# A two-way decaying scan by matrix products over channels, in place of DVE's scans, in a gated RWKV and FFN block

## The chip, the cores and the metric

One NeuronCore of one Trainium2 chip. The metric is the device time of one execution in microseconds, from which a median over several executions is taken. A profiled execution gives the rows below.

## The reference

`x` and `ctx` are 32 sequences of 128 tokens and 256 channels, float32. The attention part is a bidirectional accumulation with a decay per channel, on `k = v = ctx`, and the FFN is a gated one on fake-quantised integers.

```python
ek = exp(k); ew = exp(w)                      # w, u: one value per channel
# forward:  A_t = sum_{i<t} ew^(t-1-i) ek_i v_i ;  B_t the same without v ; backward alike
cur = exp(u + k)
wkv = (Af + Ab + cur * v) / (Bf + Bb + cur)
x = x + tanh(g_xattn) * sigmoid(layernorm(x)) * wkv
xq = fake_quant(layernorm(x))                 # one scale: the maximum over all of x
h = fake_quant(silu(xq @ wg.T) * (xq @ wu.T)) # weights fake-quantised by row; one scale for all h
x = x + tanh(g_ffn) * (h @ wd.T)
```

Two maxima over everything cut the work into three stages: attention and layernorms, then gate and up, then down.

## The kernel before

The engines' programs are written out by hand, each in its own block, and wait for each other on counting semaphores. Only the first stage and the weights' preparation are changed.

- **First stage, by groups.** A group is 4 sequences (`GS`), `GROUPS` = 8. A half (`h`) is 128 of the 256 channels, so there are 16 units of 128 partitions by 512. The loop of every engine is skewed by hand over groups (`step(g)`).
- For a unit, ACT takes `ek = exp(ctx)` (L410), POOL multiplies it by ctx (`pk`, L315), PE transposes both into PSUM so that channels are partitions and tokens lie along the free dimension (`turn_in`, L867), ACT makes `cur` (L421), and DVE runs two scans of 1024 elements, forward (L664) and backward (L666). POOL clears the borders (`zero`, L325). PE transposes cur and both scans back, accumulating the three in one bank (`turn_out`: L881, L883, L885), once for e and once for p.
- DVE makes the denominator `(1 + exp(-norm x)) * sum_e` (L677), ACT its reciprocal by Ln and Exp (L443, L446), DVE the `mixed` term (L689), POOL adds it to x (`residual`, L334).
- **Layernorms.** `stats1` and `join1` (L623, L632) on x before the residual, `rstd1` on POOL (L342 to L348), `exp_z` on ACT (L432, four instructions a group). After the residual `stats2`, `join2` (L643, L652), `rstd2` on POOL (L354 to L361), `normalise` on ACT (L457, four a group), `turn_z` on PE (L903), `keep_z` on ACT (L466), `peak_z` on DVE (L696). All of it is inside the same skewed loop, one to three groups behind.
- **Weights.** `weight_scales` (DVE L611 to L613), `quantise_weights` (L474), `cast_weights` (L482) on ACT, `turn_weights` (PE, L918), `keep_weights` (ACT L491). Gate and up are done in the first groups, down behind the gate and up stage.
- **Behind the last group** `global_peak` (DVE L751, PE L944, DVE L754 to L756) gives the scale, `quantise_x` (DVE L766) and `cast_x` (ACT L547) the integers, and L976 is the first gate matmul. L1012 is the down product, L841 its scaling, L990 the product of `ones` with a diagonal, the only float32 matmul that is no transpose.

Of the kernel before, what the change touches and what calls it, by code (L numbers as in the profile page):

```python
# [40 lines left out]

def gated_rwkv_ffn(nc, x, ctx_kv, g_xattn, g_ffn, w, u, clip_x, clip_down, w_gate, w_up, w_down, out):
# [14 lines left out]
    SCW = 2 * UNIT + 2  # L57
    assert T == P and IR == P // 2 and UNIT == 512 and CH == 2 and GROUPS >= 5

    with ExitStack() as stack:  # L60
# [5 lines left out]

# [10 lines left out]
        ones = sb("ones", [P, P])  # L77
        small = sb("small", [P, 64])
# [5 lines left out]

        hidden = sb("hidden", [P, BLOCKS * HB])
        at = [0]

        def part(cols):
            at[0] += cols
            assert at[0] <= BLOCKS * HB  # L90
            return hidden[:, at[0] - cols:at[0]]

        ctx_all = part(SEQS * C)
        ek = part(2 * UNIT).rearrange("p (s n) -> p s n", s=2)
        pk = part(2 * UNIT).rearrange("p (s n) -> p s n", s=2)
        cur = part(4 * UNIT).rearrange("p (s q n) -> p s q n", s=2, q=2)
        scans = part(2 * 2 * SCW).rearrange("p (s d n) -> p s d n", s=2, d=2)

        decay = [tile.rearrange("p (h n) -> p h n", h=CH) for tile in (
            part(CH * 2 * UNIT), xq[:, :, :, :, :].rearrange("p a b c d -> p (a b c d)").bitcast(F32))]  # L100
        ez = part(GC)

        den = part(2 * UNIT).rearrange("p (s n) -> p s n", s=2)
        lnd = part(UNIT)
        rden = part(2 * UNIT).rearrange("p (s n) -> p s n", s=2)

        late = silu_out[:, :, :].rearrange("p s n -> p (s n)")
        mixed = late[:, 0:2 * UNIT].rearrange("p (s n) -> p s n", s=2)
        z = late[:, 2 * UNIT:2 * UNIT + GC]
        x8 = sb("x8", [P, 2, CH, 512], I8)  # L110
        h8_space = sb("h8_space", [P, 2 * HB // 4])

        z_flat = z_t[:, :, :].rearrange("p h n -> p (h n)")
        WC = KA * C
        w_nat = [z_t[:, 0, TOK - WC:TOK], z_t[:, 1, TOK - WC:TOK], h8_space[:, 0:WC]]
        w_int = sb("w_int", [P, WC], I8)
        w_intb = sb("w_intb", [P, WC], BF16)
        assert TOK - WC >= 4 * UNIT

# [6 lines left out]

        ps = stack.enter_context(nc.psum_tensor("ps", [P, 8, 512], F32))
        TURN = 6, 6, 2


# [8 lines left out]

        EVEN = (KA + 1) // 2  # L140
        ODD = KA // 2

# [4 lines left out]


# [3 lines left out]
        wu_raw = small[:, 16:20]  # L152
# [17 lines left out]
        nr2 = sb("nr2", [P, GS])  # L170
        mr2 = sb("mr2", [P, GS])
        consts = sb("consts", [P, 3, GS])
        zero_tile = sb("zero_tile", [P, 2, 2 * GS + 1])
        zeros = zero_tile[:, :, :]


# [866 lines left out]
```

## Time and profile before

| | |
|---|---|
| median of 3 runs | 245.43 us (242.9 to 245.86) |
| the profiled execution | 245.59 us, its span 243.9 us |
| busy share of the span: DVE, ACT, PE, POOL | 90%, 68%, 64%, 50% |
| first stage, until the first gate matmul | 0 to 153.0 us |
| gate and up with their maximum | 153.0 to 208.6 us |
| down product and output | 208.6 to 243.9 us |

Times in rows are microseconds from the start of the span, those of one instruction in nanoseconds where the view says so. PE is the matmul engine and PEld its weight loads. The granted TensorE clock is a share of 2.4 GHz, so that 0.50 is 1.2 GHz. A window's columns are the engine's busy time with the number of instructions in it.

### The profile page before, as it was taken

What the parts mean: (1) busy time and instruction counts of PE and PEld (TensorE: products, weight loads), DVE (VectorE), ACT (ScalarE), POOL (GpSimd) and SP (SyncE); (2) the same over time, 40 slices, a digit from 0 to 9 for tenths busy, and PEclk for the clock granted to TensorE, in tenths of its full rate; (3) what the DMA queues carried; (4) which work ended last, traced back from release to release, by engine and by line L of the source; (5) the groups of instructions that cost most, each with busy time, mean ns of one, the idle gap of its engine ahead of it and who ended that gap; (6) DMA issues with size and microseconds to landing.
All of it is one profiled execution on the core that took longest, in us unless ns stands there. A gap on an engine that the chain in (4) does not pass through costs nothing.

```text
span 243.9 us, 3531 instructions
## 1 busy us (share of the span) xinstructions
PE 156.2 (64%) x1002; PEld 113.4 (47%) x1002; DVE 219.0 (90%) x307; ACT 166.8 (68%) x220; POOL 121.4 (50%) x151
## 2 busy tenths in 40 slices
PE   0609675476726596556565622999595993689970
PEld 0409565476625485545465612434232341466640
DVE  0999999999999999999999787279999799899993
ACT  5454975929959197393772759799797788689700
POOL 7431444438465384454832740057373575008992
PEclk9955979889999978999987875699998899599995
DMA  5796566610000000000000000000000000002358
GB/s 152 217 336 198 174 203 219 220 50 4 0 0 0 0 0 0 0 0 0 0 0 0 4 0 0 0 1 0 3 0 0 0 0 0 1 3 86 129 180 293
DMA packets 16107, 15.08 MB, mean 62 GB/s; under 512 B 2016, under 2 KB 15840, under 8 KB 16096
## 3 DMA queue, kind: packets, MB, share of 16 engines
q1 hardware_dynamic: 16096, 14.95, 19.2%
q8 instruction: 5, 0.08, 0.1%
q14 instruction: 6, 0.05, 0.1%
HBM read 10.75 MB, written 4.19 MB: 61 GB/s over the span
## 4 chain that ended last, share of the span: by engine, by line
DVE 29%; issue 21%; PE 18%; POOL 14%; ACT 12%; DVEq 2%; DMA 2%; POOLq 1%; SPq 0%; ACTq 0%
DVE hidden L666 9%; PE ps L1012 8%; PE ps L976 7%; DVE hidden L664 3%; POOL rs L357 3%; POOL x_all L334 3%; ACT silu_out L567 2%; POOL hidden L387 2%; POOL hidden L315 2%; DVE h_space L823 2%; DVE h_peaks L789 2%; DMA hidden<-in_ctx 2%; POOL rs L344 2%; DVE hidden L778 2%; DVE x L766 1%
## 5 line engine op out<-in xcount | busy, mean ns | idle before, releaser
L881 PE MATMUL ps<-ident,hidden 128*128 128x128 f32 x128 | 41.4, 323 | 48.5 <-POOL hidden L325 23.7
L881 PEld LDWEIGHTS ps<-ident,hidden 128*128 128x128 f32 x128 | 21.0, 164 | 54.7 <-POOL hidden L325 43.4
L883 PE MATMUL ps<-ident,hidden 128*128 128x128 f32 x128 | 40.2, 314 | 0.0
L885 PE MATMUL ps<-ident,hidden 128*128 128x128 f32 x128 | 40.1, 313 | 0.0
L664 DVE TENSOR_TENSOR_SCAN hidden<-hidden,ps 128x1024 f32<-128x1024 f32 x16 | 36.3, 2269 | 0.0
L666 DVE TENSOR_TENSOR_SCAN hidden<-xq,ps 128x1024 f32<-128x1024 f32 x16 | 36.2, 2262 | 0.0
L443 ACT ACTIVATE hidden<-hidden 128x512 f32<-128x512 f32 x16 | 10.0, 625 | 33.9 <-DVE hidden L677 33.9
L325 POOL TENSOR_TENSOR hidden<-zero_tile 128x18 f32<-128x18 f32 x16 | 3.5, 222 | 56.7 <-DVE hidden L666 56.7
L976 PE MATMUL ps<-xq,wuT 128*128 128x512 bf16 (+1 forms) x96 | 24.8, 402 | 6.4 <-DVE hidden L778 6.2
L1012 PE MATMUL ps<-wdT,z_t 128*128 128x256 bf16 (+1 forms) x192 | 25.4, 288 | 2.6 <-ACT z_t L585 2.6
L789 DVE TENSOR_REDUCE h_peaks<-hidden (+2 forms) x24 | 26.1, 1122 | 0.6 <-POOL hidden L387 0.3
L387 POOL TENSOR_TENSOR hidden<-silu_out,up_out 128x1024 f32 x6 | 14.5, 2424 | 21.8 <-ACT up_out L571 21.8
L976 PE MATMUL ps<-xq,wgT 128*128 128x512 bf16 (+1 forms) x96 | 24.7, 401 | 0.0
L867 PE MATMUL ps<-ident,hidden 128*128 128x128 f32 x128 | 18.5, 292 | 6.4 <-ACT hidden L410 6.2
L1012 PEld LDWEIGHTS ps<-wdT,z_t 128*128 128x128 bf16 (+1 forms) x192 | 17.3, 102 | 10.7 <-issue 4.8
L585 ACT ACTIVATE z_t<-h_space 128x1024 bf16<-128x1024 int8 (+3 forms) x12 | 20.1, 1754 | 2.7 <-DVE h_space L823 2.7
L885 PEld LDWEIGHTS ps<-ident,hidden 128*128 128x128 f32 x128 | 21.3, 166 | 0.0
L883 PEld LDWEIGHTS ps<-ident,hidden 128*128 128x128 f32 x128 | 21.3, 166 | 0.0
L315 POOL TENSOR_TENSOR hidden<-hidden 128x512 f32<-128x512 f32 x16 | 20.8, 1303 | 0.6 <-ACT hidden L410 0.6
L334 POOL TENSOR_TENSOR x_all<-x_all,silu_out 128x512 f32<-128x512 f32 (+1 forms) x16 | 20.3, 1273 | 0.3
L567 ACT ACTIVATE silu_out<-ps,mix_scale 128x1024 f32<-128x1024 f32 (+1 forms) x18 | 18.3, 1022 | 3.2 <-PE ps L976 3.2
L421 ACT ACTIVATE hidden<-ps,small 128x1024 f32<-128x1024 f32 x16 | 17.7, 1103 | 3.1 <-PE ps L867 3.1
(91 smaller groups left out, 363.1 us busy)
## 6 DMA issues: line engine op xcount, KB each, us to landing
hidden<-in_ctx SPq DMA_DIRECT2D x8, 512.0 KB, 3.7
x_all<-in_x SPq DMA_DIRECT2D x8, 512.0 KB, 4.6
out<-x_all SPq DMA_DIRECT2D x16, 256.0 KB, 2.2
h_space<-in_L_ffn_w_down SPq DMA_DIRECT2D x1, 704.0 KB, 7.1
z_t<-in_L_ffn_w_gate SPq DMA_DIRECT2D x1, 640.0 KB, 6.2
z_t<-in_L_ffn_w_up SPq DMA_DIRECT2D x1, 640.0 KB, 7.4
z_t<-in_L_ffn_w_gate SPq DMA_DIRECT2D x2, 64.0 KB, 6.4
z_t<-in_L_ffn_w_up SPq DMA_DIRECT2D x2, 64.0 KB, 7.6
```

What stands on the lines that cost most here:

```text
L315: nc.gpsimd.tensor_tensor(pk[:, h, :].rearrange("p (b c) -> p b c", c=P), ek[:, h, :].rearrange("p (b c) -> p b c", c=P), seqs(ctx_all, g ...
L334: nc.gpsimd.tensor_tensor(xs, xs, mixed[:, h, :].rearrange("p (b c) -> p b c", c=P), ALU.add).then_inc(s["x1_done"], 1)
L567: nc.scalar.activation(silu_out[:, 1, 0:cols] if k % 2 else silu_even[even % 2], banks[0], ACT.Silu, scale=mix_scale[:, 0, k:k + 1]).then_ ...
L585: nc.scalar.activation(hq[:, b % 2, cols], h8[:, b % 2, cols], ACT.Copy).then_inc(s["hq_done"], 1)
L664: nc.vector.tensor_tensor_scan(scans[:, h, 0, 1:2 * UNIT + 1], decay[0][:, h, :], src, 0.0, ALU.mult, ALU.add)
L666: nc.vector.tensor_tensor_scan(scans[:, h, 1, 0:2 * UNIT][:, ::-1], decay[1][:, h, ::-1], src[:, ::-1], 0.0, ALU.mult, ALU.add).then_inc(s ...
L789: nc.vector.tensor_reduce(h_peaks[:, bass.ds(KA * b + k, 1)], hidden[:, bass.ds(b * HB + k * BT, cols)], AX.X, ALU.max, apply_absolute_val ...
L881: nc.tensor.matmul(dst, cur[:, h, q, i * T:(i + 1) * T], ident[:, :], start=True, stop=False, is_transpose=True)
L883: nc.tensor.matmul(dst, scans[:, h, 0, q * UNIT + i * T:q * UNIT + (i + 1) * T], ident[:, :], start=False, stop=False, is_transpose=True)
L885: last = nc.tensor.matmul(dst, scans[:, h, 1, q * UNIT + i * T + 1:q * UNIT + (i + 1) * T + 1], ident[:, :], start=False, stop=True, is_tr ...
L976: last = nc.tensor.matmul(dst, wT[:, h, k * P:k * P + rows_], xq[:, sl, j, h, :], start=(h == 0), stop=(h == CH - 1))
L1012: last = nc.tensor.matmul(ps[:, 4 * sl + i, j * C:(j + 1) * C], lhs, rhs, start=(k == 0 and j == 0), stop=(k == KA - 1), skip_group_check= ...
```

## The change

The scans, their transposes and the loop by groups go. In their place:

1. **ctx first.** SP issues w, u and g_x, then the 8 loads of ctx into a ring of 6 slots of 512 KB, with the loads of x from the fifth of ctx on. The first four matrix loads stand between the last four loads of x. The loads have a semaphore of their own by slot and by group.
2. **Reversal.** For each group PE multiplies by `flip`, an anti-diagonal matrix, two float32 matmuls of 512 columns; ACT takes exp out of PSUM into `ek`, laid out by channel (`c q b`), and DVE, no longer POOL, multiplies (`product`), both with a strided PSUM operand.
3. **The matrices.** ACT makes a row of 255 powers for every channel (`lag_weights`), stores 261 KB to DRAM, and SP loads it back as 32 chunks of 8 channels (`load_lags`), 128 by 128 float32 for each channel, every partition starting one element later.
4. **The product.** `accumulate(j)` is one float32 matmul a channel with the channel's matrix as weights, 256 in all, streaming 128 columns: 64 that are wanted and the next channel's 64, overwritten by the next matmul. Six banks are in turn, so chunk j waits for the mix of chunk j-6.
5. **All x statistics before the first denominator.** DVE runs the 8 products, then `stats1` for 8 groups, then waits for all `exp_z`. `exp_z` writes with a stride of 32 elements.
6. **Denominator and mix** by chunk (256 elements), reciprocal and residual by pair of chunks (512 elements), the residual over all 32 sequences.
7. **Weights inside the chunks**: PE turns them after chunks 10, 14 and 20; ACT and DVE have them at fixed pairs. Down's are no longer done behind gate and up.
8. **The second layernorm behind the last residual**, for all 8 groups, except half of its statistics (`early_stats`).

```diff
+    CK = 8
+    CHUNKS = C // CK
+    PAIRS = CHUNKS // 2
+    SLOTS = 6
+    BANKS = 6
+            def load_lags(j):
+                before = GROUPS + j - SLOTS
+                if before < GROUPS:
+                    sp.wait_ge(s["ctx_back"], before + 1)
+                else:
+                    sp.wait_ge(s["ab_done"], before - GROUPS + 1)
+                src = bass.AP(lag_dram, j * CK * LAGS, [[1, P], [LAGS, CK], [1, T]])
+                sp.dma_start(lag_tile(j), src).then_inc(ring_in[(GROUPS + j) % SLOTS], 16)
...
+            for g in range(GROUPS):
                 load_ctx(g)
+                if g >= SLOTS - 2:
+                    load_x(g - SLOTS + 2)
+            sp.wait_ge(s["lag_stored"], 16)
+            for j in range(CHUNKS):
+                load_lags(j)
+                if j < 4:
+                    load_x(GROUPS - 4 + j)
+                if j == 5:
+                    load_weights(0)
+                if j == 9:
+                    load_weights(1)
+                if j == 14:
+                    load_weights(2)
...
+            def exp_k(g):
+                act.wait_ge(s["ctx_back"], g + 1)
+                nc.scalar.activation(group(ek, g), turned(g).rearrange("p (b c) -> p c b", c=C), ACT.Exp).then_inc(s["ek_done"], 1)
...
+            for m in range(PAIRS):
+                reciprocal(m)
+                if m == 4:
+                    quantise_weights(0)
+                    cast_weights(0)
+                if m == 6:
+                    keep_weights(0)
+                    quantise_weights(1)
+                    cast_weights(1)
+                if m == 8:
+                    keep_weights(1)
+                if m == 9:
+                    quantise_weights(2)
+                    cast_weights(2)
+                if m == 11:
+                    keep_weights(2)
+                if m == 12:
+                    exp_clips()
             tanh_ffn()
-            keep_z(last_g - 1)
+            normalise(0)
+            for g in range(1, GROUPS):
+                normalise(g)
+                keep_z(g - 1)
...
+            for g in range(GROUPS):
+                product(g)
+            for g in range(GROUPS):
+                stats1(g)
+            dve.wait_ge(s["tanh_done"], 1)
+            denominator(0)
+            denominator(1)
+            done = 0
+            for m in range(PAIRS):
+                if m + 1 < PAIRS:
+                    denominator(2 * m + 2)
+                mix(2 * m)
+                if m + 1 < PAIRS:
+                    denominator(2 * m + 3)
+                mix(2 * m + 1)
+                if m == 3:
+                    weight_scales(0)
+                if m == 5:
+                    weight_scales(1)
+                if m == 8:
+                    weight_scales(2)
...
+                if m > 9:
+                    n = min(6, SEQS - done)
+                    early_stats(done, n)
+                    done += n
+            late_stats(0)
+            late_stats(1)
+            for g in range(2, GROUPS):
+                late_stats(g)
+                peak_z(g - 2)
+            peak_z(GROUPS - 2)
+            peak_z(GROUPS - 1)
...
+            def reverse(g):
+                pe.wait_ge(ring_in[g % SLOTS], 16 * (g // SLOTS + 1))
+                wait(pe, s["pk_done"], g - 2)
+                for i in range(2):
+                    half = slice(i * GC // 2, (i + 1) * GC // 2)
+                    last = nc.tensor.matmul(turned(g)[:, half], flip[:, :], ring[g % SLOTS][:, half], start=True, stop=True)
+                last.then_inc(s["ctx_back"], 1)
+            def accumulate(j):
+                n = GROUPS + j
+                pe.wait_ge(ring_in[n % SLOTS], 16 * (n // SLOTS + 1))
+                if j == 0:
+                    pe.wait_ge(s["pk_done"], GROUPS)
+                wait(pe, s["mix_done"], j - BANKS + 1)
+                for c in range(CK):
+                    end = min(c + 2, CK)
+                    last = nc.tensor.matmul(ps[:, j % BANKS, c * 2 * SEQS:end * 2 * SEQS], lag_tile(j)[:, c, :],
+                                            ekp[:, (j * CK + c) * 2 * SEQS:(j * CK + end) * 2 * SEQS], start=True, stop=True)
+                last.then_inc(s["ab_done"], 1)
...
+            for j in range(CHUNKS):
+                accumulate(j)
+                if j == 10:
+                    turn_weights(0)
+                if j == 14:
+                    turn_weights(1)
+                if j == 20:
+                    turn_weights(2)
+            for g in range(GROUPS):
+                turn_z(g)
```

## Rows read from the trace of the kernel before

**Rows 1.** The page: busy time by engine, and the chain by line.
```profile
PE 156.2 (64%) x1002; PEld 113.4 (47%) x1002; DVE 219.0 (90%) x307; ACT 166.8 (68%) x220; POOL 121.4 (50%) x151
...
DVE hidden L666 9%; PE ps L1012 8%; PE ps L976 7%; DVE hidden L664 3%; POOL rs L357 3%; POOL x_all L334 3%; ACT silu_out L567 2%; POOL hidden L387 2%; POOL hidden L315 2%; DVE h_space L823 2%; DVE h_peaks L789 2%; DMA hidden<-in_ctx 2%; POOL rs L344 2%; DVE hidden L778 2%; DVE x L766 1%
```

**Rows 2.** Window over the loop by groups: PE, PEld, DVE, ACT, POOL, clock.
```profile
13.00:141.00 128.00, 78.34 (x568) 71.83 (x568) 124.52 (x190) 85.88 (x140) 63.98 (x106) 0.88 0.20 65
```

**Rows 3.** Groups by line: count, busy us, mean ns, idle before.
```profile
L664 DVE TENSOR_TENSOR_SCAN hidden<-hidden,ps 128x1024 f32<-128x1024 f32 x16 | 36.3, 2269 | 0.0
L666 DVE TENSOR_TENSOR_SCAN hidden<-xq,ps 128x1024 f32<-128x1024 f32 x16 | 36.2, 2262 | 0.0
L421 ACT ACTIVATE hidden<-ps,small 128x1024 f32<-128x1024 f32 x16 | 17.7, 1103 | 3.1 <-PE ps L867 3.1
L778 DVE SCALAR_TENSOR_TENSOR hidden<-ps,mix_scale,silu_out 128x1024 f32 x4 | 5.1, 1273 | 0.0
L334 POOL TENSOR_TENSOR x_all<-x_all,silu_out 128x512 f32 x8 | 10.2, 1273 | 0.3
```

**Rows 4.** The page's DMA queue: packets, MB, share of 16 engines' time.
```profile
q1 hardware_dynamic: 16096, 14.95, 19.2%
```

**Rows 5.** Window with the queue full; last columns: clock, DMA share, GB/s.
```profile
12.00:18.30 6.30, 0.47 (x2) 0.47 (x3) 6.26 (x10) 3.12 (x6) 2.34 (x6) 0.60 1.07 336
```

**Rows 6.** Timeline of the start: start, length, engine, line.
```profile
1.24 0.42 SPq L238 DMA_DIRECT2D hidden<-in_ctx  x1
...
5.42 0.63 ACT L410 ACTIVATE hidden<-hidden 128x512 f32<-128x512 f32 x1 [0.15 <-DMA hidden<-in_ctx]
...
11.31 1.40 DVE L623 BATCH_NORM_STATS2 bn<-x_all 128x6 f32<-128x256 f32 x4
...
15.22 2.06 ACT L432 ACTIVATE hidden<-x_all,mr,nr 128x256 f32<-128x256 f32 x4
```

**Rows 7.** Timeline: PE's only float32 product that is no transpose.
```profile
207.62 0.92 PE L990 MATMUL ps<-down_diag,ones 128*128 128x128 f32 x4
```

**Rows 8.** Windows: PE idle, then dense float32 transposes; clock third from the end.
```profile
130.00:132.70 2.70, 0.21 (x2) 0.00 (x0) 2.70 (x3) 0.02 (x1) 0.47 (x3) 0.99 0.00 0
132.80:135.80 3.00, 3.00 (x14) 3.00 (x15) 1.90 (x3) 2.74 (x6) 2.84 (x5) 0.50 0.00 0
136.10:138.00 1.90, 1.90 (x18) 1.74 (x16) 1.86 (x10) 1.45 (x3) 0.52 (x1) 1.00 0.02 4
```

**Rows 9.** Timeline of one unit: denominator, Ln, Exp, mix.
```profile
131.98 0.67 DVE L677 SCALAR_TENSOR_TENSOR hidden<-hidden,ps 128x512 f32<-128x512 f32 x1
...
134.08 0.75 DVE L689 SCALAR_TENSOR_TENSOR silu_out<-ps,small,hidden 128x512 f32<-128x512 f32 x1 [0.30 <-issue]
```

**Rows 10.** Timeline of a weight's scales, quantising and cast.
```profile
17.39 1.73 DVE L611 TENSOR_REDUCE w_scale<-z_t 128x6 f32<-128x1536 f32 x1
...
19.59 2.50 ACT L474 ACTIVATE w_int<-z_t,w_inv 128x256 int8<-128x256 f32 x6 [1.79 <-DVE w_inv L613]
...
43.47 1.48 ACT L482 ACTIVATE w_intb<-w_int 128x1536 bf16<-128x1536 int8 x1
```

**Rows 11.** Timeline from the last residual to the first gate matmul.
```profile
142.66 0.38 DVE L652 BATCH_NORM_AGGREGATE mv<-bn 128x2 f32<-128x6 f32 x4
...
145.01 2.07 ACT L457 ACTIVATE silu_out<-x_all,mr,rs 128x256 f32<-128x256 f32 x4 [2.74 <-POOL mr L361]
...
147.52 1.22 DVE L696 TENSOR_REDUCE peaks<-silu_out 128x1 f32<-128x1024 f32 x1
...
150.40 1.42 DVE L766 TENSOR_SCALAR x<-z_t,small 128x1024 int8<-128x1024 f32 x2 [0.16 <-DVE small L756]
...
151.19 2.00 ACT L547 ACTIVATE xq<-x 128x1024 bf16<-128x1024 int8 x2
...
153.03 1.91 PE L976 MATMUL ps<-xq,wgT 128*128 128x512 bf16 x4
...
153.28 1.02 ACT L466 ACTIVATE z_t<-ps 128x1024 f32<-128x1024 f32 x1
```

More of the change, by code:

```diff
@@ new lines, in gated_rwkv_ffn, with lag_tile @@
+        at = 2 * SEQS * C
+        ring = [hidden[:, at + i * GC:at + (i + 1) * GC] for i in range(SLOTS)]
+        assert at + SLOTS * GC <= BLOCKS * HB and CK * T == GC
+        def lag_tile(j):
+            return ring[(GROUPS + j) % SLOTS].rearrange("p (g t) -> p g t", t=T)
+        z_all = hidden[:, 0:SEQS * C]
+        z_flat = z_t[:, :, :].rearrange("p h n -> p (h n)")
+        ez = z_flat.rearrange("p (c b) -> p c b", b=SEQS)
+        late = silu_out[:, :, :].rearrange("p s n -> p (s n)")
@@ L203, in gated_rwkv_ffn, with half_bank @@
         out_v = out.rearrange("b t c -> t b c")
-        def ok(g):
-            return not isinstance(g, int) or 0 <= g < GROUPS
-        def iterate(engine, step, last_skew, ahead, stop=None):
-            first, end = last_skew, GROUPS - ahead
-            for g in range(first):
-                step(g)
-            with engine.Fori(first, end) as g:
-                step(g)
-            for g in range(end, stop or GROUPS + last_skew):
-                step(g)
-        def do_early(early, g, h):
-            for work, m in early.get((g, h), ()) if isinstance(g, int) else ():
-                work(m)
         def seqs(tile, first, n):
-            return tile[:, bass.ds(first * C, n * C)].rearrange("p (b c) -> p b c", c=C)
+            return tile[:, first * C:(first + n) * C].rearrange("p (b c) -> p b c", c=C)
+        def half_bank(j, q):
+            return ps[:, j % BANKS, :].rearrange("p (c q b) -> p q c b", q=2, b=SEQS)[:, q, :, :]
         @block.sync
@@ L448, in normalise, with reciprocal @@
[L448 to L455 removed]
+            def reciprocal(m):
+                act.wait_ge(s["den_done"], 2 * m + 2)
+                wait(act, s["rden_done"], m)
+                nc.scalar.activation(lnd, den[:, m % 2, :], ACT.Ln).then_inc(s["ln_done"], 1)
+                act.wait_ge(s["ln_done"], m + 1)
+                wait(act, s["mix_done"], 2 * m - 2)
+                nc.scalar.activation(rden[:, m % 2, :], lnd, ACT.Exp, scale=-1.0).then_inc(s["rden_done"], 1)
@@ L642, in stats2, with early_stats, late_stats @@
+            def early_stats(first, n):
+                dve.wait_ge(s["x1_done"], PAIRS // 2)
+                for i in range(first, first + n):
+                    stats2(i, 0)
+            def late_stats(g):
+                dve.wait_ge(s["x1_done"], PAIRS)
                 for i in range(GS):
-                    last = nc.vector.bn_stats(bn2[:, i, :], xs[:, i, :])
+                    last = stats2(g * GS + i, 1)
                 last.then_inc(s["bn2_done"], 1)
-                wait(dve, s["bn2_done"], g + 1)
```

563 lines of the change are left out of this document (186 added, 377 removed).

## The prediction

> **What bounds the kernel now.** Read the page's busy times and its chain first [rows 1]: DVE is busy 90% of the span, and the heaviest pieces of the chain in the first stage are its scans. The window over the loop by groups [rows 2] shows DVE busy for 124.5 of 128 us, PE for 78, ACT for 86. The groups by line [rows 3] name the work: 16 forward and 16 backward scans, 36.3 + 36.2 = 72.5 us, more than half of the loop. So DVE sets the pace of the loop, one group in about 16 us, and everything of both layernorms is hidden beside it. The loop ends near 141 us, and the first gate matmul starts at 153.03 us [rows 11]. What follows isn't changed, except that down's weights are prepared earlier. Before, that ran beside DVE's last maxima (table: that stage ends at 208.6), so I count nothing for it. The question is thus when the first gate matmul starts. I follow the new kernel's chain to it.
>
> **Step 1, loads and reversal.** The first ctx load was issued at 1.24 and used at 5.42, 4.2 us later [rows 6]. Three small issues now stand ahead of it, about 0.5 us each, so it lands near 6.4. With the queue full, 336 GB/s flowed [rows 5], so 524,288 B take 1.56 us. The eighth ctx load is the 11th transfer (three of x are between): 6.4 + 10 x 1.56 = 22.0 us. The 12th, x's fourth group, lands at 23.6. For the reversal I need the price of a float32 matmul that is no transpose. The two of L990 appear as four records, so one is two pairs of load and matmul. They take 0.92 us in all, the clock falling between them [rows 7]. Dense transposes start every 3.00 / 14 = 0.213 us at clock 0.50 and every 1.90 / 18 = 0.106 us at 1.00 [rows 8]. The four records fit that spacing: 0.11 + 0.16 + 0.21 and the last one's 0.42. So I take 0.109 us fast and 0.213 slow for a pair of 128 columns, and four times that for 512. A group's reversal is 4 such pairs, 1.75 us fast, and keeps up with the loads: the last ends at 23.8. Exp (1.10) and product (1.27), by the operations on 1024 elements out of PSUM [rows 3], end at 26.2. Until then DVE is mostly idle.
>
> **Step 2, statistics and exp_z, alone on the path.** DVE now runs stats1 eight times, 1.40 [rows 6] + 0.38 (the same aggregation in [rows 11]) and gaps, 1.9 each, to 41.4. POOL's part lies between the first join and exp_z; for the second layernorm ACT came 1.97 us behind the join [rows 11], so with a gap exp_z begins at 30.2. It needs 2.06 a group [rows 6]: 8 x 2.07 = 16.6 with gaps, so 46.8 us. Before, both were hidden beside the scans. PE does chunks 0 to 5 meanwhile, then waits, as all six banks are full. The stride of the exps and of the product's operands is shown by no row here. I take no surcharge, since the trace has rows only for plain operands, and keep double as the other end. For exp_z that would be +16.6 us.
>
> **Step 3, the first mix.** Two denominators of 256 elements. L677 takes 0.67 for 512 and L689 0.75 [rows 9]; half the elements cost between half and all of it. I take 0.40 and 0.48, nearer to half, since DVE's time grows with elements (1.27 for 1024 [rows 3]). The mix began 2.10 us after the denominator's start, 1.43 behind its end [rows 9]. First mix done: 46.8 + 0.8 + 1.43 + 0.48 = 49.5 us. Now PE may start chunk 6.
>
> **Step 4, 26 chunks.** A chunk is 8 channels x 2 pairs = 16 pairs: 1.75 us fast, 3.41 slow. DVE needs 2 x (0.40 + 0.48) = 1.8 a pair of chunks, up to 3.3 with the reciprocal's wait and the early statistics, ACT 1.3, POOL 1.27 to 1.9: all within PE's 3.5. So PE is the pace, if the matrices arrive.
> The clock: it was still 0.99 in 2.7 us of idleness, 0.50 in the next 3.0 us of dense work, and 1.00 from 136.1 on [rows 8]. So after a wait of some 3 us I count 3.3 us slow (0.97 of a chunk instead of 1.9).
> The weights stop PE three times. PE stands at `turn_weights(0)` behind chunk 10. DVE does the scales only behind den and mix of chunk 9: 0.40 + 0.48 + 2.15 us [rows 10], ACT then 2.50 + 1.48 [rows 10], with waits 7.15 us after chunk 9, chunk 10 covers 1.75: wait 5.4. Behind PE's wait stand chunks 11 on, and behind them every denominator. The second is alike with keep_weights ahead, 5.6; the third has 1.75 instead of 2.50, 4.6. The 12 turns take 1.3 us of the slow stretch each time, so 2.0 us are left for 0.59 chunk.
> - chunks 6 to 10: 49.5 + 3.3 + 4.03 x 1.75 = 59.9; wait to 65.3
> - 11 to 14: + 3.3 + 3.41 x 1.75 = 74.5; wait to 80.1
> - 15 to 20: + 3.3 + 5.41 x 1.75 = 92.9; wait to 97.5
> - 21 to 31: + 3.3 + 10.41 x 1.75 = 119.0 us
>
> **The matrices' traffic** is 16.8 MB beside 15 MB of all else. Packets of 512 B don't occur alone in the trace. By bytes a chunk takes 1.56 us [rows 5]; by packets, 1024 of the 46.5 ns that a mean packet takes (19.2% of 16 x 243.9 us over 16,096 [rows 4]) on 16 engines, 2.98 us. I take the middle, 2.3. The queue has delivered all by 23.6 + 4 x 1.56 (x) + 7.0 (2.36 MB of weights) + 32 T, and PE ends 1.75 later: 38.6 + 32 T. At 2.3 that is 112.2, under 119.0, so the traffic is hidden behind PE, with slots full again after each wait; T = 2.51 us is where it is no longer.
> A rule that speaks against this: the Trainium skill, "DMA: Bandwidth & Descriptors", section "How a descriptor splits into AXI transactions", says that a descriptor not starting on 256 B fetches the bytes ahead of its start as well, which makes 16 beats of a matrix row about 20. No row here shows such a packet. By it the byte price would be 1.95 us, by bytes alone still hidden.
>
> **Step 5, the end of the first stage.** Chunk 31's denominator 0.40, then 1.8 until the mix (the early statistics stand ahead of it), two mixes 0.96: 122.2. The residual is 1.27 with plain operands [rows 3], now read with a stride; I take 1.6: 123.8. Late statistics of a group, half the elements of 1.40 [rows 6] and 0.38, 1.3: 125.1, ACT 1.97 later [rows 11]: 127.1. Now ACT has eight normalises and, ahead of the last one's end, six keeps: 8 x 2.08 + 6 x 1.03 = 22.8 us [rows 11], 149.9 us. Before this work was beside the scans and the last normalise ended at 147.08. Peak 1.2 and global peak 1.7 (147.52 to 150.40 in [rows 11]): x8 at 152.8, xq's first half 1.85 later [rows 11], 154.6 against 153.03. **Sum: +1.6 us.** DVE's 72.5 us of scans and PE's turns are gone, and come back as 16.6 us of statistics and exps, 15.6 us of waits for weights, some 45 us of matmuls, 6.5 us of slow clock and 23 us of ACT behind the last residual.
>
> The profiled execution was 245.59, 1.7 over its span of 243.9, beside a median of 245.43. So 245.4 + 1.6 = **247 us**.
>
> **The rivals.**
> - **Forecast, 0.42**: as summed, own range 241 to 254 (products out of PSUM, residual, lengths of the waits).
> - **The matrices' loads set the pace, 0.22.** For it: 128 overlapping rows out of the same 8 KB, read by 16 queues, twice as many packets as for ctx. Against: three waits in which the ring refills. It decides from T = 2.51 on. At 2.98 the end is 38.6 + 95.4 = 134.0, +15 us, 262; at half of the full queue's rate (3.12 us) 138.4, 266 us. The Trainium skill, same page, "HBM row pitch at large powers of two", saw half the rate where streams by partition went in lock step; this pitch is 4 B, and no run here shows it.
> - **TensorE keeps its full clock through the waits, 0.18.** The clock was 0.99 over 2.7 us of idleness. It would give back 4 x 1.6 us: 240.5, with short mixes 236. Against: the next stretch was at 0.50.
> - **Strides cost ACT double, 0.12.** ez ends at 63 instead of 46.8: 263 us; half of that, 255.
> - **The clock doesn't come back in the chunks, 0.06**: 23 more chunks at 3.41, +38, 285 us. The Trainium skill, "TensorE: Matmul & The Clock Gate", Part 4, says that the fast state doesn't engage for transposes. The trace disagrees, 1.00 over 18 of them [rows 8].
>
> **How the numbers follow.** Faster by over 2% (under 240.5; about 2% is what a measurement of this kernel can tell) takes most of the third case and the low tail of the first: 0.24. Slower by over 2% (over 250.3): the second, fourth and fifth, and a little of the first and of the third's mistakes: 0.42. Same: 0.34. The range runs from 238 to 268: it leaves out the lowest of the third case, the fifth, and the worst of the second.
>
> **What would show it.** In the changed profile: ctx's last reversal near 24 us and the last exp_z near 47 (ACT strided write: mean of L432's successor 589 ns or near double); 256 x 2 float32 matmuls at 0.109 us apart and clock 1.00 between the waits; three PE waits of 5 us ended by ACT's cast; DMA busy share under 1 from 50 us on and matrices landing ahead of PE (if PE waits for the DMA, the second case); the last residual near 124 us, then ACT without a gap for 23 us; the first gate matmul near 154.6. The forecast is wrong if DVE, not PE, has no idleness between 60 and 119 us, or if the loads do.

## The result, and the profile after

| | before | after |
|---|---|---|
| median of the runs | 245.65 us (242.9 to 245.92, 4 runs) | 253.25 us (252.9 to 254.29, 4 runs) |
| profiled execution: span | 243.9 us | 251.7 us |
| mean granted clock over the span | 0.877 | 0.846 |

The ratio of the times is given as 1.0343, with a 95% interval of 1.0262 to 1.0423 (the two medians alone make 1.031): the changed kernel is slower by 7.6 us. The forecast was 247 us, and no change was its direction. The time lies inside both ranges, the forecast's own (241 to 254) and the whole one (238 to 268), but at the upper edge of the first. Below, where slow executions, at a lower granted clock, are among the four of a kernel, the first time leaves them out and the one "over all four" has them in. The kernel before, run again beside the experiments, had medians from 243.16 to 245.63 us, so a difference of 1% between two totals says little.

The page of the changed kernel, busy time by engine, then the chain by line, then three groups that the change brought:

```profile
PE 172.4 (68%) x1030; PEld 124.4 (49%) x1034; DVE 163.6 (65%) x343; ACT 154.9 (62%) x198; POOL 99.2 (39%) x117
...
PE ps L800 19%; ACT z_t L401 8%; PE ps L908 7%; PE ps L874 7%; ACT hidden L420 6%; DMA hidden<-in_ctx 5%; PE ps L787 4%; ACT z_t L427 3%; ACT w_int L435 2%; ACT silu_out L523 2%; DVE h_space L750 2%; POOL hidden L362 2%; ACT w_intb L443 2%; DVE h_peaks L716 2%; PE ps L812 2%
...
L800 PE MATMUL ps<-hidden 128*128 128x128 f32 (+1 forms) x512 | 68.3, 302 | 14.6 <-DVE silu_out L615 8.1
L345 POOL TENSOR_TENSOR x_all<-x_all,silu_out 128x512 f32<-128x512 f32 x16 | 24.4, 1525 | 62.4 <-DVE silu_out L615 62.4
L606 DVE SCALAR_TENSOR_TENSOR h_space<-z_t,ps 128x256 f32<-128x256 f32 x32 | 13.1, 416 | 45.6 <-PE ps L800 37.8
```

Beside [rows 1], DVE fell from 90% to 65%, and its scans, at the head of the old chain, are gone. The new chain begins with PE's products over the channels (L800, 19%) and the exponentials of ACT (L401, 8%). That is the shift the prediction described: DVE waits for PE (37.8 us at L606), and no longer the other way round.

The timeline of PE, from the chunks to the first gate matmul, carries most of the reading. Its columns are start, length of a stretch without a gap, engine and line, shapes, count, and the idle time ahead of it with what ended it:

```profile
36.05 2.00 PE L800 MATMUL ps<-hidden 128*128 128x128 f32 x16 [1.31 <-DMA hidden<-lag_w]
39.38 2.00 PE L800 MATMUL ps<-hidden 128*128 128x128 f32 x16 [1.33 <-DMA hidden<-lag_w]
42.69 2.00 PE L800 MATMUL ps<-hidden 128*128 128x128 f32 x16 [1.31 <-DMA hidden<-lag_w]
52.74 11.65 PE L800 MATMUL ps<-hidden 128*128 128x128 f32 x80 [8.06 <-DVE silu_out L615]
69.65 1.47 PE L812 MATMUL ps<-ident_b,w_intb 128*128 128x128 bf16 x12 [5.26 <-ACT w_intb L443]
70.91 9.33 PE L800 MATMUL ps<-hidden 128*128 128x128 f32 x64
85.53 1.46 PE L812 MATMUL ps<-ident_b,w_intb 128*128 128x128 bf16 x12 [5.29 <-ACT w_intb L443]
86.78 11.84 PE L800 MATMUL ps<-hidden 128*128 128x128 f32 x96
103.12 1.46 PE L812 MATMUL ps<-ident_b,w_intb 128*128 128x128 bf16 x12 [4.50 <-ACT w_intb L443]
104.37 22.15 PE L800 MATMUL ps<-hidden 128*128 128x128 f32 x176
...
161.16 1.58 PE L874 MATMUL ps<-xq,wgT 128*128 128x512 bf16 x3 [3.24 <-ACT xq L503]
```

The x16 rows are one chunk each. Chunks 3 to 5 wait for their matrices, without harm, since PE then waits 8.06 us for the first mix anyway. The x80, x64, x96 and x176 rows are chunks 6 to 10, 11 to 14, 15 to 20 and 21 to 31. Each of the three turns of the FFN weights stands behind a wait of about 5 us for ACT's cast, 15.05 us together. The last product ends at 126.52. (Three of four records of the first gate matmul are there; its operand is ready at 160.7.)

In the rows each float32 product of L800 appears twice, as two pairs of a weight load and a matmul, so a chunk of 8 channels is x16. "Pair" below means one of these.

Windows of 10 us over the four stretches show the clock (third from the end: 1 is full speed, 0.50 the lower level):

```profile
54.00:64.00 10.00, 10.00 (x74) 0.80 0.80 209
64.00:74.00 10.00, 4.74 (x30) 0.71 0.51 152
74.00:84.00 10.00, 6.24 (x51) 0.94 0.98 252
84.00:94.00 10.00, 8.47 (x68) 0.83 0.32 81
94.00:104.00 10.00, 5.50 (x51) 0.92 0.85 236
104.00:114.00 10.00, 10.00 (x71) 0.74 0.43 110
114.00:124.00 10.00, 10.00 (x92) 1.00 0.58 154
```

The clock falls behind each wait and comes back within the next stretch. Only the last window, which follows no wait, is at full clock throughout. (Its x92 counts every pair that touches the window; from start to start a pair takes 0.112 us, as the next experiment shows.) The last column also shows that the queue is half empty between the waits (81 and 110 GB/s in two windows), because SP stands at its ring of buffers. The matrices aren't what PE waits for here.

### The profile page after: what moved, and what is told of

It is laid out like the page before. It is cut to its first block, busy times and chain, and to the rows that moved or that the text cites. A ratio compares the mean times of both kernels' runs of the same rounds, so it can differ in the third digit from the quotient of the medians.

```text
span 251.7 us, 3143 instructions
## 1 busy us (share of the span) xinstructions
PE 172.4 (68%) x1030; PEld 124.4 (49%) x1034; DVE 163.6 (65%) x343; ACT 154.9 (62%) x198; POOL 99.2 (39%) x117
## 4 chain that ended last, share of the span: by engine, by line
PE 41%; ACT 28%; DVE 14%; DMA 5%; issue 5%; POOL 4%; DVEq 1%; SPq 0%; POOLq 0%; ACTq 0%
PE ps L800 19%; ACT z_t L401 8%; PE ps L908 7%; PE ps L874 7%; ACT hidden L420 6%; DMA hidden<-in_ctx 5%; PE ps L787 4%; ACT z_t L427 3%; ACT w_int L435 2%; ACT silu_out L523 2%; DVE h_space L750 2%; POOL hidden L362 2%; ACT w_intb L443 2%; DVE h_peaks L716 2%; PE ps L812 2%
## 5 line engine op out<-in xcount | busy, mean ns | idle before, releaser
L800 PE MATMUL ps<-hidden 128*128 128x128 f32 (+1 forms) x512 | 68.3, 302 | 14.6 <-DVE silu_out L615 8.1
L800 PEld LDWEIGHTS ps<-hidden 128*128 128x128 f32 x512 | 67.5, 218 | 16.0 <-issue 11.4
L345 POOL TENSOR_TENSOR x_all<-x_all,silu_out 128x512 f32<-128x512 f32 x16 | 24.4, 1525 | 62.4 <-DVE silu_out L615 62.4
L606 DVE SCALAR_TENSOR_TENSOR h_space<-z_t,ps 128x256 f32<-128x256 f32 x32 | 13.1, 416 | 45.6 <-PE ps L800 37.8
L823 PE MATMUL ps<-ident,hidden 128*128 128x128 f32 x64 | 14.8, 408 | 16.4 <-ACT hidden L420 16.4
L787 PE MATMUL ps<-hidden,flip 128*128 128x512 f32 x32 | 16.4, 664 | 8.4 <-DMA hidden<-in_ctx 8.4
L401 ACT ACTIVATE z_t<-x_all,mr,nr 128x256 f32<-128x256 f32 x32 | 19.1, 782 | 4.9 <-POOL mr L327 4.9
L823 PEld LDWEIGHTS ps<-ident,hidden 128*128 128x128 f32 x64 | 11.8, 213 | 19.1 <-ACT hidden L420 19.1
L420 ACT ACTIVATE hidden<-x_all,mr,rs 128x256 f32<-128x256 f32 x32 | 16.4, 592 | 4.4 <-POOL mr L339 4.4
L362 POOL TENSOR_TENSOR hidden<-h_space 128x1024 f32 x6 | 14.5, 2409 | 9.6 <-ACT h_space L527 9.6
L874 PEld LDWEIGHTS ps<-xq,wuT 128*128 128x128 bf16 (+1 forms) x96 | 8.6, 103 | 19.1 <-DVE hidden L705 8.9
L705 DVE SCALAR_TENSOR_TENSOR hidden<-ps,mix_scale,silu_out 128x1024 f32<-128x1024 f32 (+3 forms) x12 | 13.2, 1101 | 5.8 <-ACT silu_out L523 5.6
```

The costliest lines, as they stand in the source:

```text
L345: nc.gpsimd.tensor_tensor(xs, xs, mixed[:, m % 2, :, :].rearrange("p c b -> p b c"), ALU.add).then_inc(s["x1_done"], 1)
L362: nc.gpsimd.tensor_tensor(hidden[:, bass.ds((b + half) * HB + k * BT, BT)], silu_even[i % 2], up_even[i % 2], ALU.mult).then_inc(s["h_even ...
L401: last = nc.scalar.activation(ez[:, :, n], xs[:, i, :], ACT.Exp, scale=nr1[:, n:n + 1], bias=mr1[:, n:n + 1])
L420: last = nc.scalar.activation(z_all[:, n * C:(n + 1) * C], xs[:, i, :], ACT.Identity, scale=rs2[:, n:n + 1], bias=mr2[:, n:n + 1])
L787: last = nc.tensor.matmul(turned(g)[:, half], flip[:, :], ring[g % SLOTS][:, half], start=True, stop=True)
L800: last = nc.tensor.matmul(ps[:, j % BANKS, c * 2 * SEQS:end * 2 * SEQS], lag_tile(j)[:, c, :], ekp[:, (j * CK + c) * 2 * SEQS:(j * CK + en ...
```

## The experiments

The rows above name four suspects: the waits for the weights, the clock behind them, the exponentials' stride with the statistics ahead of it, and the traffic of the matrices. Each was tried alone; then the ones that gave something were put together. The diffs are against the changed kernel. Where an experiment adds lines, the line numbers in its rows shift: L800 becomes L804, L812 becomes L814 or L816.

**The turns of the weights later.**

```
-                if j == 10: turn_weights(0)
-                if j == 14: turn_weights(1)
-                if j == 20: turn_weights(2)
+                if j == 14: turn_weights(0)
+                if j == 19: turn_weights(1)
+                if j == 24: turn_weights(2)
```

> The changed kernel with one edit: PE turns the weights behind chunks 14, 19 and 24 instead of 10, 14 and 20, when their cast is ready. Theory (the chain through PE): the three waits for ACT's cast, 5.3 + 5.3 + 4.5 us in the changed kernel's profile, go, and with them the slow stretches behind them, 5 to 7 us; PE's last chunk ends near 105 instead of 126.5 us and the median is near 232 us. Rival (the matrices' loads are about to set the pace): PE then waits for loads instead, and little more than half is won, about 243. Rival (DVE and ACT set the pace, PE's waits are free): no change, 253.

Measured: 236.89 us, 237.13 over all four (234.26 to 238.36), ratio to before 0.9654 [0.9509, 0.9799]. This one edit turns the slower kernel into a faster one. PE's timeline:

```profile
52.68 19.13 PE L800 MATMUL ps<-hidden 128*128 128x128 f32 x144 [8.08 <-DVE silu_out L615]
71.65 0.83 PE L812 MATMUL ps<-ident_b,w_intb 128*128 128x128 bf16 x12
75.55 10.77 PE L800 MATMUL ps<-hidden 128*128 128x128 f32 x80 [3.07 <-DMA hidden<-lag_w]
...
86.83 9.10 PE L800 MATMUL ps<-hidden 128*128 128x128 f32 x80
95.76 0.83 PE L812 MATMUL ps<-ident_b,w_intb 128*128 128x128 bf16 x12
96.43 12.67 PE L800 MATMUL ps<-hidden 128*128 128x128 f32 x112
```

The three waits are gone, and a turn takes 0.83 us instead of 1.47, since it now runs at full clock. The chunks end at 109.1 instead of 126.52. The row of 9.10 us, with no wait ahead of it, gives the price at full clock: from its start to the next turn's, 95.76 - 86.83 for 80 pairs, a pair takes 0.112 us and a chunk 1.79. One new wait appeared, 3.07 us for matrices, with a slower stretch behind it (10.77 us for the five chunks that take 9.10 next). SP's own timeline shows why: it stood from 61.5 to 68.4 us at the load of w_down (L263), which waits until ACT has quantised the first weight, and all further matrices are queued behind it. Wait and slower stretch make 4.7 us, which is about what lies between the expected 232 and the measured 237.

**The waits kept, the clock kept up**, with products of no use in them.

```
+                wait(pe, s["w_stored"], m)
+                for _ in range((22, 16, 18)[m]):
+                    nc.tensor.matmul(ps[:, TURN + 1, 0:P], ones[:, :], ident[:, :], start=True, stop=True)
                 pe.wait_ge(s["w_cast"], m + 1)
-                wait(pe, s["w_stored"], m)
```

> The changed kernel, but PE fills the waits for the weights' cast with 22, 16 and 18 float32 products of ones with the identity into a bank that the transposes overwrite. The waits stay as long as they are. Theory (after a wait of 5 us PE runs at 1.2 GHz for some us): the chunks behind each wait run at clock 1.00 at once; 2.2, 1.1 and 2.5 us of slow chunks and 3 x 0.4 of slow transposes are saved, 246 us. Rival (the chunks behind a wait are slow because of matrix loads or bank waits): no change, 253, or slower if the fillers delay a turn.

Measured: 248.46 us (246.56 to 248.6), ratio 1.0146 [1.0042, 1.025]. PE's timeline:

```profile
63.83 5.13 PE L808 MATMUL ps<-ident,ones 128*128 128x128 f32 x44
69.26 0.84 PE L814 MATMUL ps<-ident_b,w_intb 128*128 128x128 bf16 x12 [0.30 <-ACT w_intb L443]
69.94 7.31 PE L800 MATMUL ps<-hidden 128*128 128x128 f32 x64
...
83.23 10.88 PE L800 MATMUL ps<-hidden 128*128 128x128 f32 x96
...
99.29 19.82 PE L800 MATMUL ps<-hidden 128*128 128x128 f32 x176
```

From the end of a stretch to the turn it is 5.26, 5.30 and 4.50 us, as long as before, but the work behind it is done at full clock: turns and chunks take 0.84 + 7.31, 10.88 and 19.82 instead of 1.47 + 9.33, 11.84 and 22.15. That is 2.65 + 1.6 + 2.9 = 7.1 us that the three idle waits had cost on top of themselves. So with PE idle for the same 5 us the clock drops, and with PE kept at work it doesn't. Of the gain, 2 to 3 us are given back later: xq's conversion starts 7.4 us earlier than in the changed kernel (152.24 instead of 159.64), the end only 4.9. The first gate and up matmuls tell: 1.98, 1.91 and 1.91 us (the first with all four of its records) instead of 1.58 (three of four records), 1.69 and 1.03, so the low clock lasts longer into them.

**Half as many columns.** Only a channel's own 64 columns stream, not its neighbour's too, so that a product writes 64 columns.

```
-                    end = min(c + 2, CK)
+                    end = c + 1
```

> The changed kernel, but each channel's matmul streams only its own 64 columns instead of 128. Theory (a pair of weight load and matmul is bound by the weight load of 128 float32 columns, 107 ns at full clock, and the columns are free beside it): pairs stay 0.11 us apart and the time stays within 1% of 253, unless the clock needs the columns. Rival (the matmul's columns are the bound): pairs come 0.06 to 0.08 us apart, chunks take 1.1 us, and the matrices' loads at about 1.9 us a chunk set the pace: near 248. Rival (fewer columns keep the clock at 0.50): chunks take 3.4 us, 285.

Measured: 284.67 us (283.85 to 285.81), ratio 1.166 [1.1546, 1.1775]. PE's timeline, and then windows of the same kernel (clock third from the end):

```profile
52.81 17.30 PE L800 MATMUL ps<-hidden 128*128 128x64 f32 x80 [5.35 <-DVE silu_out L615]
...
118.58 37.75 PE L800 MATMUL ps<-hidden 128*128 128x64 f32 x176
```

```profile
52.00:70.00 18.00, 17.19 (x80) 0.50 0.55 149
...
130.00:150.00 20.00, 20.00 (x96) 0.50 0.30 79
```

Half the columns take longer: 37.75 us instead of 22.15 for 176 pairs. The granted clock stays at 0.50 through 20 us of unbroken work, where the 128-column stretch was at 1.00 (114 to 124 us above). A pair takes 0.2145 us (37.75 / 176). Transposes of 128 columns at clock 0.50 came 0.213 us apart [rows 8], so at half clock half the columns aren't cheaper; what they would cost at full clock no run shows, since the clock never rose in this stage. The neighbour's 64 columns, whose sums the neighbour's own product overwrites, are useless in themselves, but with them the stage runs at full clock. The prediction's last rival, the clock that doesn't come back (285 us), is what happens with 64 columns; with 128 it doesn't happen. That its time is met to within a microsecond is luck: it was 38 us on top of 247, and here 31 us come on top of 253, because the waits for the casts are shorter (3.63, 3.67 and 2.87 us) and some of the changed kernel's chunks were slow already.

**The first two groups' statistics between the products**, so that exp_z can start sooner.

```
-            for g in range(GROUPS): product(g)
-            for g in range(GROUPS): stats1(g)
+            for g in range(6): product(g)
+            stats1(0); product(6); stats1(1); product(7)
+            for g in range(2, GROUPS): stats1(g)
```

> The changed kernel, but DVE takes the statistics of groups 0 and 1 into its waits between the last products (behind the sixth and the seventh). Theory (exp_z stands alone on the path, ACT's pace of 2.39 us a group counts from its start at 30.7): it starts at 25.9, right behind the last exp of ctx, and the first mix comes 3.5 to 4.8 us earlier: 249. Rival (the last x load or DVE's last statistics end it): under 2 us, 252.

Measured: 249.34 us (248.15 to 250.99), ratio 1.022 [1.0109, 1.0332]: 3.9 us less than the changed kernel. exp_z starts at 26.80 instead of 30.69, and PE goes on at 49.06 instead of 52.74:

```profile
49.06 10.74 PE L804 MATMUL ps<-hidden 128*128 128x128 f32 x80 [3.69 <-DVE silu_out L615]
```

The head of the stage is on the path, nearly one for one.

**The exponentials stored plainly.** ACT writes ez in the order of the sequences, and DVE reads it with the stride.

```
-        ez = z_flat.rearrange("p (c b) -> p c b", b=SEQS)
+        ez = z_flat.rearrange("p (b c) -> p c b", c=C)
```

> The changed kernel, but exp(-norm x) is stored sequence by sequence, so that ACT writes plain rows and DVE's denominators read it with a stride of 256 elements instead of in rows of 32. Theory (the stride of ACT's writes costs 0.19 us an instruction, 782 against 589 ns, and DVE has slack): exp_z takes 16.6 instead of 19.1 us, the denominators may take longer beside PE, the median falls by about 2.5 us to 250.5. Rival (DVE's strided read costs as much or more, and shows): 253 or slower.

Measured: 253.82 us (252.98 to 254.64), ratio 1.0425 [1.0355, 1.0494] to its own runs of before. Groups by line between 28 and 56 us, the changed kernel first, then this one (count | busy us, mean ns | idle):

```profile
L401 ACT ACTIVATE z_t<-x_all,mr,nr 128x256 f32<-128x256 f32 x32 | 19.1, 782 | 4.9 <-POOL mr L327 4.9
```

```profile
L401 ACT ACTIVATE z_t<-x_all,mr,nr 128x256 f32<-128x256 f32 x32 | 15.8, 591 | 4.8 <-POOL mr L327 4.8
L606 DVE SCALAR_TENSOR_TENSOR h_space<-z_t,ps 128x256 f32<-128x256 f32 x8 | 4.5, 583 | 6.3 <-ACT z_t L401 4.4 <-PE ps L800 1.9
```

The strided write costs ACT 191 ns for 256 values, 32%; turned round, it costs DVE 583 instead of 416 ns. ACT is 3.3 us sooner done, PE goes on at 49.94 instead of 52.74, and a lead of 3.05 us is there at xq's conversion (156.59 instead of 159.64). Then it is lost. The first gate and up matmuls of this kernel, in PE's timeline:

```profile
158.10 1.58 PE L874 MATMUL ps<-xq,wgT 128*128 128x512 bf16 x3 [3.23 <-ACT xq L503]
159.47 1.92 PE L874 MATMUL ps<-xq,wuT 128*128 128x512 bf16 x4
161.18 1.92 PE L874 MATMUL ps<-xq,wgT 128*128 128x512 bf16 x4
162.88 1.44 PE L874 MATMUL ps<-xq,wuT 128*128 128x512 bf16 x4
164.16 1.03 PE L874 MATMUL ps<-xq,wgT 128*128 128x512 bf16 x4
```

Up to 164 us four bands are at half clock here (up to 1.92 us for one, instead of 1.03), in the changed kernel two (1.58 and 1.69). Behind a wait near 180 us two more are slow (1.91 and 1.74) that take 1.03 there. From xq's start to the end of the program it is 94.8 us here and 92.1 in the changed kernel. So the stride costs ACT 3.3 us, and turning it round brings PE on 2.8 us sooner, but the total doesn't show it. The rival hit the total, not the reason: PE's waits for the weights grew by only 0.5 us (5.43 + 5.47 + 4.67).

**Half the matrices.** Four of the eight matrices of a chunk are loaded and each is used twice, so half of the channels are computed with another channel's powers.

```
-                src = bass.AP(lag_dram, j * CK * LAGS, [[1, P], [LAGS, CK], [1, T]])
-                sp.dma_start(lag_tile(j), src).then_inc(ring_in[(GROUPS + j) % SLOTS], 16)
+                src = bass.AP(lag_dram, j * CK * LAGS, [[1, P], [LAGS, CK // 2], [1, T]])
+                sp.dma_start(lag_tile(j)[:, 0:CK // 2, :], src).then_inc(ring_in[(GROUPS + j) % SLOTS], 16)
...
-                    last = nc.tensor.matmul(ps[:, j % BANKS, c * 2 * SEQS:end * 2 * SEQS], lag_tile(j)[:, c, :],
+                    last = nc.tensor.matmul(ps[:, j % BANKS, c * 2 * SEQS:end * 2 * SEQS], lag_tile(j)[:, c % (CK // 2), :],
```

> The changed kernel, but each chunk loads only 4 of its 8 matrices and PE uses each twice, so that half the matrix traffic (8.4 MB) goes and part of the result is computed with the wrong channel's powers. Theory (the loads are hidden behind PE): within 1.5 us of 253. Rival (the loads set or share the pace): several us faster, up to 15 if PE was waiting for them at each chunk.

Measured: 252.28 us (250.95 and 253.61), 254.19 over all four (to 256.04), ratio 1.0456 [1.038, 1.0531]. PE's timeline:

```profile
52.88 10.77 PE L800 MATMUL ps<-hidden 128*128 128x128 f32 x80 [14.12 <-DVE silu_out L615]
```

With half the traffic the time stays about where it was. PE is done sooner with chunks 0 to 5, waits 14.12 us instead of 8.06, and goes on at 52.88 (52.74); the three waits for the casts are 5.26, 5.29 and 4.49 us as before. The profiled execution is 2.5 us shorter, 1.6 of it in the chunks, which have no wait less and recover their clock a little sooner. In the changed kernel the traffic is hidden.

**Three moves together**: the turns behind chunks 14, 19 and 24; the statistics as above; and w_down's load behind chunk 17's instead of 14's, so that SP isn't held by it.

> Three moves together, nothing computed otherwise: the turns behind chunks 14, 19 and 24, the statistics of groups 0 and 1 among the products, and w_down's loads issued behind the 18th matrix load instead of the 15th. With the late turns alone PE still waited 3.1 us for a matrix load that stood behind SP's wait for w_down's buffer, and ran slow after it. Theory (PE's chain, waits add up): 237.1 less 3.6 for the statistics, less 3.1 for the wait and 1.8 for the slow chunks: 229. Rival (the loads themselves are late once PE doesn't wait): 234.

Measured: 227.81 us (227.67 to 229.27), ratio 0.9368 [0.9305, 0.943]. It beats the kernel before by 6% and the changed one by 25 us. PE's timeline:

```profile
48.69 17.89 PE L804 MATMUL ps<-hidden 128*128 128x128 f32 x144 [4.01 <-DVE silu_out L615]
66.41 0.83 PE L816 MATMUL ps<-ident_b,w_intb 128*128 128x128 bf16 x12
67.08 9.45 PE L804 MATMUL ps<-hidden 128*128 128x128 f32 x80
...
77.04 9.10 PE L804 MATMUL ps<-hidden 128*128 128x128 f32 x80
...
86.64 12.69 PE L804 MATMUL ps<-hidden 128*128 128x128 f32 x112
```

From 48.69 to 99.33 PE has no gap at all, 416 pairs and three turns in 50.6 us. In the changed kernel the same work took from 52.74 to 126.52, 73.8 us. Of the 23.2 us between them, 15.05 are waits and 8.1 the clock, which is low for longer in the changed kernel.

**More on top of it, three times.** First, 36 products of no use ahead of chunk 6, and the last group's normalisation on DVE:

> The three moves, and two more: PE runs 36 filler products before chunk 6, in its 8 us of waiting for the first mixes, and DVE instead of ACT makes the last group's second normalisation (four instructions) and its maximum ahead of the one before. Theory: the fillers save the slow first chunks, 2.5 us; ACT behind the last residual has one normalise less, 2 to 3 us; 229 less 5: 224. Rival (another queue is next at either place, DVE's pace behind the first mix, or the keeps at the end): 227 to 229.

Measured: 228.36 us, 229.09 over all four (226.52 to 231.59), ratio 0.9435 [0.9354, 0.9516]: nothing won. The useless products ran until 51.57, 2.9 us longer than the wait; behind them 144 pairs took 16.19 instead of 17.89 us, so keeping PE at work kept the clock once more, but PE's end moved from 99.33 to 100.1. The normalisation on DVE did win something: from PE's end to xq's conversion it is 32.0 us instead of 33.1, 1.2 where 2 to 3 had been expected. Second and third, the plain store of the exponentials on top of the three moves, without and with 12 such products:

> The kernel with three moves (the turns of the FFN weights behind chunks 14, 19 and 24, the third weight load behind chunk 17, the first two groups' statistics between the products), with the exponentials also stored in the order of the sequences. If the stride of ACT's writes costs path time here, exp_z is about 3.3 us shorter than the 20.2 us from its first to its last in the three moves' trace, the chunks go on at about 45.5 us instead of 48.7, nothing waits for weights behind them, and the time is 227.8 - 3 = about 225 us. The rival, by the run of that store order alone (its gate product began 3.06 us earlier and its span was 0.3 us shorter): what is won ahead of the feed-forward part is given back there at half clock, and the time stays at 227 to 228 us.

> The same, with 12 products of no use (ones by the identity, into a spare bank) ahead of chunk 6, from the fifth group's exponential on, so that the wait for the first mixes is mostly filled. If the idle stretch ahead of chunk 6 is what drops the granted clock there, the chunks behind it start at full clock, and 144 pairs take about 16.2 us as behind 36 such products, in place of the 17.9 us of the three moves: 1.7 us less than the run beside it, about 223 us. Rival: 12 are too few or the gain is given back later, and the two are alike, within 1 us.

Measured: 226.44 us (226.4 and 226.49), 228.54 over all four (to 230.8), and 226.47 us, 227.45 over all four (225.19 to 228.81; ratio 0.9261 [0.916, 0.9362]). They are within 1.4 us of the three moves' 227.81, taken on another occasion: neither is shown to be better. PE's timeline without the 12 products, and, of the same kernel, its DMA engines between 50 and 90 us (busy tenths in 40 slices of 1 us, and what was moved):

```profile
46.77 8.96 PE L804 MATMUL ps<-hidden 128*128 128x128 f32 x64 [2.26 <-DVE silu_out L615]
56.27 9.19 PE L804 MATMUL ps<-hidden 128*128 128x128 f32 x80 [0.55 <-DMA hidden<-lag_w]
...
72.53 3.81 PE L804 MATMUL ps<-hidden 128*128 128x128 f32 x32 [1.04 <-DMA hidden<-lag_w]
```

```profile
DMA  9999999999999999999999997999999999999999
...
DMA packets 21745, 11.63 MB, mean 291 GB/s; under 512 B 1072, under 2 KB 21485, under 8 KB 21741
```

PE goes on 1.9 us sooner (46.77 instead of 48.69), and then waits for matrices; with the 12 products it waits 1.95 + 0.36 + 0.94 + 0.51 us. Chunk 10 starts at 56.27 in the one and at 56.19 in the other, and the last product ends at 99.11 and 100.17, against 99.33 with the three moves alone. The DMA engines are busy in every slice. Up to chunk 19 the traffic has here become the bound that the prediction's second rival spoke of, and its waits eat what both edits gain ahead of it. This is read from the rows; no run takes traffic out of this kernel.

## Why the prediction was right, and where it was not

The structure held at every step; two terms were off by more than 2 us, the products with their clock and exp_z, and the sum missed by 6 us, which is all but 0.8 us of the room that the range left above the forecast. Times are the profiled execution's.

| step | predicted | measured | what it adds |
|---|---|---|---|
| 1: last product with exp(k) ends | 26.2 | 27.1 | |
| 2: exp_z begins | 30.2 | 30.7 | +0.5 |
| 2: exp_z, its length | 16.6 | 19.1 | +2.5 |
| 3: PE goes on | 49.5 | 52.74 | +3.2 in all |
| 4: waits for the weights | 5.4, 5.6, 4.6 | 5.26, 5.29, 4.50 | -0.6 |
| 4: products from chunk 6 on, with turns | 53.9 | 58.7 | +4.8 |
| 4: last product | 119.0 | 126.5 | +7.5 in all |
| 5: from there to the last residual's end | 4.8 | 4.4 | -0.4 |
| 5: from there to the first normalise | 3.3 | 3.3 | |
| 5: first to last normalise | 22.8 | 21.5 | -1.3 |
| 5: from there to xq's first half | 4.7 | 5.0 | +0.3 |
| 5: xq's first half ready | 154.6 | 160.7 | +6.1 in all |
| behind it, to the end of the span | 90.9 | 91.0 | +0.1 |

(90.9 is 243.9 - 153.03 of before.)

- **Loads and reversal** were right within a microsecond. ACT's exps behind the reversals follow each other 1.72 us apart while the loads keep up, for 1.75 counted; the price from the four records of [rows 7] carried over to real products.
- **Statistics ended** at 42.3 instead of 41.4, which is the head's lateness and nothing more.
- **exp_z** was the first mis-sized term: I took no surcharge for the stride because [rows 6] has only plain operands, and kept double as the other end. A group took 2.39 us instead of 2.07. Between ends at 0 and +16.6 us, +2.5 was near the value taken, and the plain store showed the stride alone, 3.3 us of ACT's time.
- **The waits for the weights** were right within about 0.3 us each. They were built from [rows 9] and [rows 10] alone; and the turns moved later showed that they, with the clock, make the whole difference between slower and faster.
- **The products** were the largest mis-sized term, 4.8 us. Low clock: I counted 3.3 us of it behind each of four waits, from one place in [rows 8], giving 1.6 us each. Against the lengths at full clock (9.10 us for 80 pairs, 0.1138 a pair), the four stretches with their turns lost 2.5, 2.7, 1.6 and 2.8 us, 9.6 instead of 6.5, which makes 3.1. One recovery is no measure of them all, and not even one place has a fixed price: the first stretch, behind the wait for the first mix, took 11.65 us here and 10.63, 10.74, 10.77 and 11.28 with the clock kept up further on, the statistics early, half the matrices and the plain store. Full clock: a chunk took 1.79 us from start to start, where the transposes of [rows 8] had given 1.75; over 26 chunks 0.9 us. The remaining 0.8 us isn't traced further; a part is that a stretch ends with the whole of its last product (276 ns in the median at L800), where the sum had one spacing.
- **The residual** took 1.49 to 1.54 us with a strided operand, 1273 before [rows 3]; 1.6 had been taken.
- **The tail** was ACT's, as forecast, the eight normalises with the keeps between them. From one normalise to the next it was 2.87 us (150.74 to 153.61 in ACT's timeline), where 2.08 + 1.03 had been counted: in the records an operation starts before the one ahead of it has ended, and the sum had added whole lengths. That was 1.3 us too much.
- **The matrices' traffic** was hidden as forecast, and its price overestimated: over 40 us with the engines full, 291 GB/s flow in the plain store with three moves, 1.80 us a chunk where 2.3 was taken, between the byte price of 1.56 and 2.98. By the line 38.6 + 32 T it ends at 96.2, 30 us ahead of PE's end in the changed kernel, but only 3 ahead of the 99 us of the three moves. The Trainium skill's rule in "DMA: Bandwidth & Descriptors", section "How a descriptor splits into AXI transactions", on descriptors that don't start on 256 B, gave an estimate of 1.95 us; the measured 1.80 lies between that and the byte price, and doesn't decide it. The sign "DMA busy share under 1 from 50 us on" was not met throughout (1.04 from 78 to 82 us and again from 98 to 102), and yet PE waited for no matrix there.
- **The rivals**: the clock did not stay up through the waits (0.50 from 52.7 on, and low behind each of the others), ACT didn't pay double (782 ns against 591), and the clock came back in the chunks. Two mechanisms were met elsewhere: the loads in the faster kernels, and the clock that doesn't come back with 64 columns.
- **The direction** was given as no change, at +1.6 us, though the chances themselves had slower at 0.42 ahead of the same at 0.34. The missing 6 us are 4.8 for products and clock and 3.2 for the head and exp_z, less 2 that were counted too high. The large ones point the same way: the plain price for a strided write, the spacing of transposes for products, and the one recovery seen were each at the low end of what came out. That the time is still inside 241 to 254 owes something to the 2 us in the other direction.

## What to carry to other kernels

When work is moved to an engine that then sets the pace, look at what stands in its in-order stream waiting for others: here three transposes of the weights, each standing right behind the chunk that starts the work for its cast, cost 15 us of waiting and 7 more of lowered clock, and placing them four or five chunks later turned +3.4% into -3.5%. Then ask the same of every queue behind it: the next bound was a load that held up SP's queue, and the one after that, by the rows, the queue's own throughput. Prices taken from plain operands and from a single recovery of the clock were too low here, and several of them in one sum didn't cancel: give such a term a range that reaches further up than down.

## What the runs showed of the hardware that was not expected

- **Fewer columns were slower.** Float32 pairs with 64 streaming columns ran at granted clock 0.50 in every window from 52 to 150 us, 0.2145 us each (37.75 / 176); with 128 columns they reached 1.00, 0.1138 us each (9.10 / 80). Why the clock stayed low isn't shown.
- **The clock of a later stage can take back what an earlier one gives.** From the start of xq's conversion to the end, work that is the same instruction by instruction took 92.1 us in the changed kernel, 94.8 with the plain store, 94.6 with the clock kept up, 93.4 with the three moves, 92.2 with plain store and three moves, and 91.1 with 12 useless products too. The mean granted clock over this part was 0.89 where it took 91.1 to 92.2 us and 0.86 where it took 94.6 and 94.8. More of the gate and up bands then run at half clock (1.9 us against 1.03); what decides how many isn't shown. A change worth under 3 us ahead of this stage can't be judged by the total; it has to be read where it acts.
- **Strides by engine, 4-byte values, 256 of them**: ACT's write with a step of 128 B 782 ns against 591, DVE's read of one operand with a step of 1 KB 583 against 416. POOL's addition of 512, one operand read with a step of 128 B: 1525 against 1273 [rows 3].
- **A 3.07 us wait ahead of five chunks cost 1.7 us of speed behind it**; a wait of 2.26 us (plain store and three moves) left 64 pairs at 8.96 us, against 7.26 where 12 useless products filled it.
